# Attention: two of the three low parts of U moved behind the mean's subtraction on VectorE

## The reference

```python
xn = layernorm(x) * norm1_g + norm1_b
q, k, v = split(xn @ qkv_w + qkv_b)              # 3 heads of 16
attn = softmax(q @ k.T * 16 ** -0.5 + bias)
x1 = x + roll_back((attn @ v) @ proj_w + proj_b)
h = gelu((layernorm(x1) * norm2_g + norm2_b) @ fc1_w + fc1_b)   # 192 wide
x2 = x1 + h @ fc2_w + fc2_b
```

## Time and profile before

| what | value |
|---|---|
| runs shown, us | 1921.74, 1924.59, 1933.83; median 1924.59 |
| profiled execution, us | 1921.47 |
| its span, us | 1919.8 |
| granted TensorE clock over the span | 0.961 |
| busy: PE, DVE, ACT, POOL | 90%, 83%, 80%, 65% |

### The profile page before, as it was taken

The page is one execution under the profiler, slowest core; times in us unless marked ns, Lnnn a source line. Parts: engine busy times, 40 slices in busy tenths (PEclk is TensorE's granted clock), DMA queues, the critical chain, the costliest instruction groups (busy, mean ns, idle before and its releaser), DMA issues. The chain is left out here.

```text
span 1919.8 us, 90636 instructions
## 1 busy us (share of the span) xinstructions
PE 1733.5 (90%) x38184; PEld 1054.6 (55%) x38184; DVE 1597.7 (83%) x2140; ACT 1535.9 (80%) x3090; POOL 1244.9 (65%) x1048
## 2 busy tenths in 40 slices
PE   5899999999999999999999999986999958998996
PEld 3566656565666656666665656651697943333332
DVE  6899889998999999999989899854777757888883
ACT  3788888888888888888888888875666639888891
POOL 5788888888888888888888888762355540221222
PEclk9999999999999999999999999995899975999998
DMA  4343554444443444444344444322588849999994
GB/s 116 89 115 97 152 133 115 106 107 115 100 116 99 117 102 113 109 105 113 98 116 102 117 105 106 85 59 67 134 217 215 216 119 170 245 260 253 253 268 142
DMA packets 233230, 262.27 MB, mean 137 GB/s; under 512 B 167078, under 2 KB 179910, under 8 KB 232710
## 3 DMA queue, kind: packets, MB, share of 16 engines
q1 hardware_dynamic: 217478, 217.48, 47.4%
q0 software_dynamic: 15360, 39.08, 6.8%
HBM read 160.81 MB, written 80.88 MB: 126 GB/s over the span
## 5 line engine op out<-in xcount | busy, mean ns | idle before, releaser
L425 POOL TENSOR_TENSOR shift<-const_b,qmax 113x588 bf16<-113x588 bf16 x256 | 414.1, 1618 | 214.7 <-DVE qmax L520 214.7
L512 DVE TENSOR_TENSOR Ul<-Uf 113x784 bf16<-113x784 f32 x192 | 259.8, 1379 | 0.0
L1501 POOL DMA_DIRECT2D out_rolled<-r_OUT x128 | 64.0, 504 | 268.2 <-DVE r_OUT L1601 268.2
L520 DVE TENSOR_REDUCE qmax<-ps_s 113x12 f32<-113x588 f32 x256 | 195.4, 763 | 50.3 <-PE ps_s L917 46.6
L1347 PE MATMUL conv_ps<-xin,band_now 64*64 64x448 bf16 x2688 | 203.4, 365 | 2.2 <-DVE x_low L1242 2.2
L731 ACT ACTIVATE P<-ps_t 113x588 f32<-113x588 f32 x256 | 170.0, 664 | 36.6 <-PE ps_t L969 34.3
L724 ACT COPY Uf<-ps_m 113x392 f32<-113x392 f32 x384 | 172.8, 485 | 28.7 <-PE ps_m L882 20.8
L1347 PE MATMUL conv_ps<-x_low,band_now 64*64 64x448 bf16 x1344 | 178.1, 352 | 0.0
L741 ACT COPY V<-ps_t 49x192 f32<-49x192 f32 x512 | 169.1, 330 | 9.2 <-PE ps_t L969 3.0
L984 PEld LDWEIGHTS ps_o<-P,V 113*32 113x32 f32 x6144 | 107.8, 109 | 102.7 <-ACT P L731 53.0
L762 ACT ACTIVATE G<-ps_m 128x392 f32<-128x392 f32 x256 | 113.9, 502 | 44.5 <-PE ps_m L1023 44.2
(11 more groups left out here) (246 smaller groups left out, 5339.9 us busy)
## 6 DMA issues: line engine op xcount, KB each, us to landing
xin<-rows_scratch SPq DMA_DIRECT2D x96, 236.0 KB, 3.7
XT<-x_tokens SPq DMA_DIRECT2D x64, 294.0 KB, 3.5
X<-x_windows SPq DMA_DIRECT2D x128, 147.0 KB, 3.4
RS<-rs_scratch SPq DMA_DIRECT2D x128, 147.0 KB, 3.2
XR<-x_windows SPq DMA_DIRECT2D x128, 147.0 KB, 3.2
x_scratch<-x SPq DMA_DIRECT2D x128, 147.0 KB, 3.5
y_scratch<-y POOLq DMA_DIRECT2D x96, 196.0 KB, 2.8
r_RS<-rs_scratch SPq DMA_DIRECT2D x128, 147.0 KB, 4.8
```

The costliest lines, as they stand in the source:

```text
L425: nc.gpsimd.tensor_tensor(shift[:, j % 2], e, m, ALU.mult).then_inc(S["md"], 1)
L512: nc.vector.tensor_tensor(Ul[:, r, h, :], Uf[:, r, h, :], U[0][:, r, h, :], ALU.subtract).then_inc(S["u_lo"], 1)
L520: nc.vector.tensor_reduce(qmax[:, j % 2, :].rearrange("p (b n) -> p b n", b=2), ps_s[0:R, :, 0:2 * HQ].rearrange("p b (n t) -> p b n t", t ...
```

## The change

In VectorE's step of the attention phase three of the calls stand in another order. The low part of head 1 goes from in front of subtract_mean to behind the square, and the low part of head 2 from in front of query_max(nxt, 1) to behind it. Nothing else differs: the same instructions, semaphores and values waited for.

```diff
                 normalise1(old)
                 divide(s, 0)
                 u_low(nxt, 0)
-                u_low(nxt, 1)
                 subtract_mean(prv)
                 query_max(nxt, 0)
                 divide(s, 1)
                 square(prv)
+                u_low(nxt, 1)
+                query_max(nxt, 1)
                 u_low(nxt, 2)
-                query_max(nxt, 1)
                 add_bias(prv)
```

## The result

The changed kernel takes 1965.7 us (median of 4 runs) against 1926.9 of the kernel before: a ratio of 1.0198, 95% interval 1.0172 to 1.0224. It is slower by 2%, as forecast (1966 us). One execution of the four, at 2366 us, is left out of the ratio; nothing in this text rests on it. The profiled execution has a span of 1964.1 us, 44.3 more than before.

What follows compares the result with a forecast made beforehand. No engine has much room, so the order of one step and the VectorE/GpSimd access decide. 19.72 - 0.69 + 0.31 + 1.04 = 20.38 us a step, +0.70 x 60 = +42 us: 1966 us, range 1897 to 1982.

Steps and rivals of the forecast that it cites:

- Case b: Shared SBUF access: VectorE, not held up and with its next operation following at once, keeps GpSimd behind both.
- Part 1: u_low(nxt,1) moved away from the mean: Q comes 0.69 us earlier per step, bounds 0 to 0.95.
- Q: Start of VectorE's maximum query_max(nxt,0), at 712.77 before the change, forecast at 712.08.
- Part 2: u_low(nxt,1) behind the square takes the place u_low(nxt,2) had: cost 0, bounds 0 to 0.3.
- Part 3: u_low(nxt,2) behind query_max(nxt,1) is held up by GpSimd's L442, so K comes 0.31 us later.
- K: Start of TensorE's keys_and_values of the next step, 5.88 us after Q before the change, forecast at Q+6.19.
- Part 4: add_bias pushed back, GpSimd's L407 getting in ahead: late second_residual, TensorE 1.04 us late from project on.
- A: VectorE keeps the access at the end of u_low(nxt,2): -0.42 us a step, 1899 us; chance 0.16.
- B: As A, but t_mean loses a 0.12 us race to GpSimd's L425: +0.28 us a step, 1941 us; chance 0.05.
- C: u_low(nxt,2) beats GpSimd's L442 although 0.23 us behind, K not delayed: -0.63 us a step, 1887 us; chance 0.07.
- D: The late residual eats up Part 1's gain and no more, Part 4 at 0.4: near 1926 us; chance 0.06.

Runs made afterwards that it cites:

- experiment 3: The changed kernel with VectorE's order untouched; GpSimd's squares_low also waits until u_low(nxt,2) is done: 1909.9 us, ratio 0.9899 to the kernel before.
- experiment 4: The changed kernel with its last two VectorE operations swapped, add_bias ahead of u_low(nxt,2): 2057.4 us, ratio 1.0669 to the kernel before.
- experiment 1: The changed kernel with both moved low parts behind the square, ahead of query_max(nxt,1): 1900.7 us, ratio 0.9856 to the kernel before.
- experiment 6: The kernel of experiment 1, with GpSimd's make_shift(nxt,0) also waiting for the square: 1903.3 us, ratio 0.9872 to the kernel before.
- experiment 5: The changed kernel with add_bias moved from behind u_low(nxt,2) to ahead of the square: 1911.1 us, ratio 0.9917 to the kernel before.
- experiment 2: The kernel before with only u_low(nxt,2) moved behind query_max(nxt,1): 1955.3 us, ratio 1.0133.
- experiment 7: The changed kernel with divide(prv,3) moved ahead of token_sums and token_squares: 2034.7 us, ratio 1.0543 to the kernel before.

## Why the prediction was right, point by point

- **Which operations exclude each other, and that GpSimd gets in behind a held-up VectorE.** Right, and it carried the sign. L407 took 2.22 us (2.2 forecast) and add_bias 1.85 (1.87). Experiment 3 takes the meeting away without touching VectorE's order, and the kernel turns from 2% slower to 1% faster; experiment 4 shows the same hand-over with the kinds swapped; in the steady steps of 1 and 6 an unhindered run keeps the access, for two and for three operations.
- **Case b, as the prediction states it,** is too wide. That VectorE was not held up isn't enough to keep the access. In the kernel before, 11 pairs of low parts that met L415 began with one of 0.96 us, that is, unhindered by its duration. In eight of them L415 was issued between 0.12 us ahead of the pair and 0.05 behind its start, and stayed behind both. In the other three it was issued 0.08 to 0.09 us behind the start and got in between, as in the 3.14 us pair of the earlier trace rows and here:

```profile
491.72 3.15 DVE L512 TENSOR_TENSOR Ul<-Uf 113x784 bf16<-113x784 f32 x2
```

```profile
491.81 2.23 POOL L415 TENSOR_TENSOR xhl<-xh 113x784 bf16<-113x784 f32 x1
```

In these three L450 ended 0.12 to 0.13 us behind the first low part's issue, in the eight 0.09 at most, so there may have been a short hold-up that the duration doesn't show. The first strip of experiment 6 can't be explained so: GpSimd was idle there. What decides, with VectorE not held up, isn't settled. The change itself doesn't hang on it: its square and first moved low part kept the access in all 62 strips in which L425 was waiting, and GpSimd got in behind the held-up u_low(nxt,2) in 62.

- By the Trainium skill (SBUF — State Buffer, Who interferes with whom) the one that issues second is blocked. The runs agree where the lead was 0.23 us (L442 against u_low(nxt,2)); they differ where it was 0.10: in experiment 1 L425 was issued ahead of the square and ran last of four. The step of 20.2 us that the prediction gave for this rule lies close to the 20.22 measured, but by accident: L425 took 2.98 us, behind the square and its low part, as case b has it.
- **Part 1, -0.69 us.** Right: project to Q is 8.09 us against 8.78. Where nothing behind it comes late, the step is 3% shorter, as experiments 1 and 5 show (19.05).
- **Part 2, nothing.** Right in the change. Experiment 2 shows that it isn't idle: without it L442 would come 0.9 us earlier and most of part 3 would vanish.
- **Part 3, +0.31 us.** Right: Q to the next K is 6.17 us against 5.88, +0.29.
- **Part 4, +1.04.** The term that was mis-sized: 0.90. second_residual started 1.65 us behind K instead of 1.72 (it overlapped the end of add_bias by 0.07, where I had put a gap of 0.03), the operations behind it came 0.08 early in step, and project followed the division 0.05 closer. That the division binds and the other waits of TensorE lie just inside was right: experiment 7 puts the difference at 0.07 us.
- **The sum.** A step of 20.22 instead of 20.38, so the steady part gave 36 us instead of 42. Two things that I didn't name made up for it: the first strips, 5.5 us, and 2.7 us behind the last strip's first_residual. In the first steps there is no second half of the block to work on, and TensorE waits for a low part behind a maximum at once: up to 66 us twice, 4.2 us in all, against 0.3 before. The granted clock differs too, and what it costs isn't separated from the waits: around the second of these waits it was at the lower level, 1.2 GHz, for 10.2 us (50.2 to 60.5), before for 3.4 (48.4 to 51.8). Of the 2.7 us, 0.9 lie ahead of the last second_residual and 1.9 in the phases behind, which took 599.7 to 605.3 us in the nine traces though no edit touches them. The total was right partly by luck, since these terms made up for the steady part: 44.3 us against 42 forecast.
- **Rivals.** A needed VectorE to keep the access behind u_low(2); it didn't in any of the 62 strips in which a GpSimd operation was waiting (L575 has a median of 1.85 us), and B needed the same. C needed u_low(2) to beat L442 by being issued 0.23 us behind it; it lost, as add_bias had. D had part 4 at 0.4; it was 0.90.

## What to carry to other kernels

Before moving a VectorE operation with two SBUF inputs, lay GpSimd's timeline beside it: durations that hold waiting show who meets whom, and an operation that lands just behind the start of a GpSimd one costs itself, and once more through the GpSimd operation that gets in behind it. Keeping such VectorE operations together in one unhindered run paid here (experiment 1), but look in the new trace who got the access: a GpSimd operation issued 0.16 us behind the start of such a run got in after its first operation (experiment 6, first strip). Put behind the last risky one nothing that another engine waits for. Price an edit by all that it pushes back, in the first steps of a pipeline too.

## What was not expected of the hardware

- Three VectorE operations in a row kept GpSimd out for 2.7 us, though GpSimd's was issued before them (experiment 1).
- In a kernel with shorter steps TensorE mostly stopped more often with no semaphore waited for, for 0.4 us and more: in steady steps once in the kernel before (19.7 us) and once in the changed one (20.2), 11 times in experiment 1, 14 in 3 and 10 in 6, but only 5 times in experiment 5, whose modal step is 19.05 us too, and 5 times in experiment 2 (20.07). The stops ended 1.26 to 1.64 us behind the landing of a packet of the instruction queue. Of an expected gain of 42 us experiment 1 kept 27.
- A stand of TensorE of some 2.2 us once per step was followed in some steps by a granted clock of 0.92 and 1.4 us more of busy time (experiment 4). A long stop could cost more than itself in the same way: one of 1.3 us in experiment 3 (at 456.24) was followed by 6.8 us at 1.2 GHz, in the interval of 22.8 us.
